# Seven sum levels instead of five and a single scale for the down weights in an attention + mixture-of-experts layer

## The reference, cut to what matters

```python
# B, T, C = 16, 512, 256; 16 heads of 16; 32 experts of width 128, top 8
x = layernorm(x + attention(x))        # q, k, v, rope, causal softmax, projection, biases
logits = x @ gate_w.T                  # x as (8192, 256)
top_w, top_idx = top_k(softmax(logits), 8)
top_w = top_w / top_w.sum(-1)
for e in range(32):                    # comb[t, e] = top_w where e is chosen, else 0
    g, u = split(x @ gate_up_w[e].T)
    acc += (u * silu(g)) @ down_w[e].T * comb[:, e]
out = layernorm(x + acc)               # layernorm without scale and bias
```

## Time and profile before

| | |
|---|---|
| runs | 2085.57, 2093.41, 2096.18 us; median 2093.41 |
| the profiled execution | 2096.7 us, of it 2094.9 from the first to the last instruction |
| mean granted TensorE clock | 0.950 of full speed |
| busy | PE 1763.9 us (84%), VectorE 1573.7 (75%), ScalarE 1288.3 (61%), GpSimd 1192.8 (57%) |
| DMA | 494.32 MB, 236 GB/s on the mean |

### The profile page before, as it was taken

The page is one execution under the profiler, slowest core; times in us unless marked ns, Lnnn a source line. Parts: engine busy times, 40 slices in busy tenths (PEclk is TensorE's granted clock), DMA queues, the critical chain, the costliest instruction groups (busy, mean ns, idle before and its releaser), DMA issues. The chain is left out here.

```text
span 2094.9 us, 54004 instructions
## 1 busy us (share of the span) xinstructions
PE 1763.9 (84%) x17245; PEld 1244.8 (59%) x17245; DVE 1573.7 (75%) x3519; ACT 1288.3 (61%) x2994; POOL 1192.8 (57%) x1158
## 2 busy tenths in 40 slices
PE   3899888988898889888987978988889889899960
PEld 2455544555455445454554868877767778788750
DVE  4788888887887888877875535745777679688887
ACT  1556665665565455554554857876767677787740
POOL 1002465446434654455444677777777777777770
PEclk8899999999999999999998989999999999999985
DMA  4455776677656665667754856778998899799966
GB/s 140 112 156 150 228 253 212 202 232 237 212 164 215 223 209 173 214 221 258 232 186 153 306 186 217 234 248 314 339 330 276 282 317 332 267 325 345 313 207 220
DMA packets 244743, 494.32 MB, mean 236 GB/s; under 512 B 46787, under 2 KB 150485, under 8 KB 235232
## 3 DMA queue, kind: packets, MB, share of 16 engines
q1 hardware_dynamic: 168256, 302.81, 46.3%
q0 software_dynamic: 54528, 159.49, 20.5%
q10 hardware_dynamic: 21696, 28.58, 4.0%
HBM read 279.66 MB, written 229.44 MB: 243 GB/s over the span
## 5 line engine op out<-in xcount | busy, mean ns | idle before, releaser
L1307 ACT ACTIVATE pT<-ps 128x512 f32<-128x512 f32 (+2 forms) x992 | 647.3, 694 | 331.0 <-PE ps L1090 253.7
L921 POOL DMA_INDIRECT x_sorted<-xhl,idx x512 | 520.2, 1016 | 469.4 <-DVE xhl L1745 229.2
L1659 DVE TENSOR_REDUCE mn<-ps 128x1 f32<-128x512 f32 (+3 forms) x704 | 412.2, 631 | 47.4 <-PE ps L1064 45.1
L1156 PE MATMUL ps<-pT,gu_hi 128*128 128x128 f16 (+1 forms) x1792 | 387.4, 238 | 60.7 <-ACT pT L1307 59.6
L1157 PE MATMUL ps<-pT,gu_hi 128*128 128x128 f16 (+1 forms) x1792 | 386.9, 237 | 0.0
L1158 PE MATMUL ps<-pT,gu_lo 128*128 128x128 f16 (+1 forms) x1792 | 379.6, 236 | 0.2 <-issue 0.2
L938 POOL DMA_INDIRECT y_tokens<-work,yidx x248 | 264.1, 1065 | 75.0 <-issue 55.3
L1062 PE MATMUL ps<-stacks 96*128 96x512 bf16 (+3 forms) x1024 | 271.9, 310 | 41.3 <-DMA stacks<-qk_parts 18.8
L1088 PE MATMUL ps<-stacks 99*128 99x512 bf16 (+3 forms) x1024 | 283.1, 306 | 24.8 <-ACT pT L1307 21.0
L1156 PEld LDWEIGHTS ps<-pT,gu_hi 128*128 x1792 | 176.5, 99 | 94.2 <-issue 73.1
L1090 PE MATMUL ps<-maskk,identb 128*128 128x128 bf16 x1024 | 221.6, 222 | 0.0
(11 more groups left out here) (235 smaller groups left out, 3610.8 us busy)
## 6 DMA issues: line engine op xcount, KB each, us to landing
stacks<-y_tokens SPq DMA_DIRECT2D x64, 1024.0 KB
stacks<-qk_parts SPq DMA_DIRECT2D x128, 192.0 KB
qk_parts<-pbuf SPq DMA_DIRECT2D x31, 768.0 KB, 4.5
stacks<-qk_parts SPq DMA_DIRECT2D x128, 128.0 KB
attention<-yev ACTq DMA_DIRECT2D x64, 256.0 KB
x_sorted<-pads_h SPq DMA_DIRECT2D x66, 160.0 KB
pT<-x_sorted SPq DMA_DIRECT2D x64, 160.0 KB
pbuf<-x_sorted SPq DMA_DIRECT2D x62, 160.0 KB
```

What stands on the lines that cost most here:

```text
L921: pool.indirect_dma_start(xsort[g][:, :], bass.IndirectOffsetOnAxis(ap=at, axis=0), xhl_rows[:, t, :], None).then_inc(s_scat, 16)
L1156: mmul(o, w_hi[k], x_hi[k], start=k == 0, stop=False)
L1307: return nc.scalar.activation(o, i, f, **k)
L1659: V.tensor_reduce(mn[:, tt, h0:h0 + nh], ps[:, odd_bank("max", at, m), 0:nh * n].rearrange("p (a n) -> p a n", a=nh), axis=AX.X, op=ALU.ma ...
```

## The change

- `LEVELS` has seven levels, of 4, 4, 2, 2 batches in group 0 and 2, 1, 1 in group 1. By `level_pairs` group 0 has 80 blocks of 256 rows instead of 112, group 1 16 as before; the 32 lie in the level of batches 8 to 11, whose blocks run in steps 72 to 104. The number of blocks and steps stays at 288 and 144. By `plan` the levels' first tiles come at steps 50, 82, 107, 120, 138, 148 and 153 instead of 50, 82, 114, 139 and 153, and the last tile at step 156 instead of 160.
- The down weights get one scale for all columns: VectorE takes the largest absolute value of each expert's rows (one more reduction in `measure`), multiplies the 32 by `mm` in iteration 8 and finds the largest of all with one transpose. ScalarE multiplies the rows by the scale (instead of VectorE). In the sums the two operations L1931 and L1934 become one.
- Batch 14's end, in iteration 15, has a table `LAST` of its own: numerators at place 3 (8 before), reciprocals out at 5 (6), division at 13 (12), inverse root at 13 (20), mean column 17 (20), normalisation 18 (22), x1's transposes 23 and 24 (24 and 25), the high and low copies of x1 both at 31 (26 and 29).
- The clears of group 0 go out in every other place of iterations 13 and 14.
- `first_row` of the table moves from x1T into `prep`, whose layout changes with it.

```diff
--- before.py
+++ after.py
@@ -88,11 +87,12 @@
...
 PREP_K = 2
+TOP = 16384.0
 
 
 BLK, UNIT = 256, 128
 GROUPS = ((0, 12), (12, 16))
-LEVELS = ((0, 4), (4, 8), (8, 12), (12, 14), (14, 16))
+LEVELS = ((0, 4), (4, 8), (8, 10), (10, 12), (12, 14), (14, 15), (15, 16))
 NG = len(GROUPS)
...
@@ -266,8 +266,11 @@
...
 
+LAST = dict(EACH, num=3, rec_out=5, divide=13, rsqrt=13, mean=17, norm=18, split=31, lower=31, x1=(23, 24), x1_out=(23, 24))
+
+
 def slots(i):
-    return LATE if i >= B else EACH
+    return LATE if i >= B else LAST if i == B - 1 else EACH
 
...
@@ -342,8 +345,8 @@
...
                         take(i, "gu", p + E * stage - 1)
-                    if stage == 1 and p in (2, 3):
-                        take(i, "fin", p - 2)
+                    if stage == 1 and p == 3:
+                        take(i, "fin", 0)
                 if place == 0 and (i, e) in TABLE_OUT:
...
@@ -470,7 +472,6 @@
...
         room, paired, sofar, twice, ended, ind, share = (eq[:, k * BINS[0]:(k + 1) * BINS[0]] for k in range(7))
-        first_row = eq[:, 7 * BINS[0]:8 * BINS[0] + 1]
         lane = sb("lane", [P, 5 * NLANE[0]])
...
@@ -486,12 +487,14 @@
...
 
-        prep = sb("prep", [P, 3 * C + 3 * E + 8])
-        mxd, rinvb, rwide = (prep[:, k * C:(k + 1) * C] for k in range(3))
-        mm = prep[:, 3 * C:3 * C + E]
-        mgu = prep[:, 3 * C + E:3 * C + 3 * E].rearrange("p (e m) -> p e m", e=E)
-        mx2 = prep[:, 3 * C + 3 * E:3 * C + 3 * E + 4].rearrange("p (r m) -> p r m", r=2)
-        rcp = prep[:, 3 * C + 3 * E + 4:3 * C + 3 * E + 8].rearrange("p (r m) -> p r m", r=2)
+        HEAD = 2 * C + 64 + BINS[0] + 8
+        prep = sb("prep", [P, HEAD + 3 * E + 8])
+        mxd, rwide = prep[:, 0:E], prep[:, C:C + P]
+        first_row = prep[:, 2 * C + 64:2 * C + 64 + BINS[0] + 1]
+        mm = prep[:, HEAD:HEAD + E]
+        mgu = prep[:, HEAD + E:HEAD + 3 * E].rearrange("p (e m) -> p e m", e=E)
+        mx2 = prep[:, HEAD + 3 * E:HEAD + 3 * E + 4].rearrange("p (r m) -> p r m", r=2)
+        rcp = prep[:, HEAD + 3 * E + 4:HEAD + 3 * E + 8].rearrange("p (r m) -> p r m", r=2)
         first_parts = pT[1][:, :, :].rearrange("p h t -> p (h t)").bitcast(BF16).rearrange("p (a r t) -> p a r t", r=2, a=3)
...
@@ -810,7 +810,7 @@
...
                         wait(sp, s_ys[k], stored(last_of(k, 2 * LEVEL_END[l])))
-                wait(sp, s_cmb, 7 * (q - NYG) + 3)
+                wait(sp, s_cmb, 6 * (q - NYG) + 3)
                 rows = ytok[q * P * TOPK:(q + 1) * P * TOPK, :].rearrange("(p k) c -> p k c", k=TOPK)
...
@@ -818,9 +818,9 @@
...
                     wait(sp, s_x1s, 16 * NB)
-                    wait(sp, s_rcb, 1)
+                    wait(sp, s_mid, 8)
                     wait(sp, s_dlo, E // 2)
-                wait(sp, s_cmb, 7 * (q - 2) + 5)
+                wait(sp, s_cmb, 6 * (q - 2) + 4)
                 sp.dma_start(x1r[:, q % 2, :], x1_dram[b, t * P:(t + 1) * P, :]).then_inc(s_x1r[q % 2], 16)
...
@@ -843,8 +843,9 @@
...
 
-                if i == GROUPS[0][1] + 1 and 0 <= e - SLOT_TAILS < E:
-                    clear_tail(0, e - SLOT_TAILS)
+                at = (i - NB + 3) * STEPS + e
+                if i < NB and 0 <= at < 2 * E and at % 2 == 0:
+                    clear_tail(0, at // 2)
                 if i >= NB and 0 <= (i - NB) * STEPS + e - LATE_TAILS < E:
...
@@ -1015,17 +1016,10 @@
...
                     xpose4(k, lambda j: rows_gu(n % 2)[:, j % 2, (j // 2) * P:(j // 2) * P + P]).then_inc(s_str, 1)
-                if stage == 1 and e in (2, 3):
-                    if e == 2:
-                        pe.wait_ge(s_dm, E)
-                        k = odd.take(s_mid, 1, "fin", 0)
-                    else:
-                        pe.wait_ge(s_mid, 4)
-                        k = odd.take(s_rb, 1, "fin", 1)
-                    src = (mxd, rwide)[e - 2]
-                    for j in range(2):
-                        last = nc.tensor.transpose(ps[:, k, j * P:(j + 1) * P], src[:, j * P:(j + 1) * P], ident[:, :])
-                    last.then_inc(s_fin, 1)
+                if stage == 1 and e == 3:
+                    pe.wait_ge(s_mid, 3)
+                    k = odd.take(s_mid, 5, "fin", 0)
+                    nc.tensor.transpose(ps[:, k, 0:P], rwide, ident[:, :]).then_inc(s_fin, 1)
 
...
@@ -1325,15 +1319,16 @@
...
                     actv(products(n, 1)[:, 0, :], rows_dn(n % 2), ACT.Copy, scale=mm[:, n:n + 1]).then_inc(s_dev, 1)
-                    if n >= 2:
-                        act.wait_ge(s_dm, n - 1)
-                    actv(sizes(n % 2), rows_dn(n % 2), ACT.Abs, scale=mm[:, n:n + 1]).then_inc(s_dev, 1)
                     if n + 2 < E:
-                        act.wait_ge(s_dev, 2 * n + 2)
+                        act.wait_ge(s_dev, n + 1)
+                        act.wait_ge(s_dm, n + 1)
                         load_rows(act, n + 2)
-                if stage == 1 and e == 3:
-                    act.wait_ge(s_fin, 2)
-                    actv(rinvb, ps[:, odd_bank("fin", 1), 0:C], ACT.Copy).then_inc(s_rb, 1)
+                n = e - 4
+                if stage == 1 and 0 <= n < E // 2:
+                    act.wait_ge(s_mid, 8)
+                    act.wait_ge(s_dev, E)
+                    wait(act, s_dlo, n - 1)
+                    actv(scaled(n % 2), products(2 * n, 2), ACT.Copy, scale=rinv[:, 1:2]).then_inc(s_dsc, 1)
                 n = e - 5
...
@@ -1572,6 +1567,9 @@
...
                     V.reciprocal(rcp[:, r, :], mgu[:, e, :]).then_inc(s_sv, 1)
+                    dve.wait_ge(s_drow[r], 16 * (e // 2 + 1))
+                    V.tensor_reduce(mxd[:, e:e + 1], rows_dn(r), axis=AX.X, op=ALU.max,
+                                    apply_absolute_value=True).then_inc(s_dm, 1)
                     V.scalar_tensor_tensor(out=mm[:, e:e + 1], in0=mgu[:, e, 0:1], scalar=4.0, in1=mgu[:, e, 1:2],
...
@@ -1585,31 +1583,24 @@
...
 
-                n = e + E * stage - 1
-                if 0 <= n < E:
-                    dve.wait_ge(s_dev, 2 * n + 2)
-                    if n > 0:
-                        dve.wait_ge(s_dm, n)
-                    V.tensor_tensor(mxd, sizes(n % 2), mxd if n else sizes(0), ALU.max).then_inc(s_dm, 1)
                 if stage == 1 and e == 2:
+                    dve.wait_ge(s_dm, E)
+                    dve.wait_ge(s_mm, E)
+                    V.tensor_tensor(mxd, mxd, mm, ALU.mult).then_inc(s_mid, 1)
+                    dve.wait_ge(s_mid, 1)
+                    V.tensor_reduce(rinv[:, 0:1], mxd, axis=AX.X, op=ALU.max).then_inc(s_mid, 1)
+                    dve.wait_ge(s_mid, 2)
+                    V.tensor_copy(rwide, rinv[:, 0:1].to_broadcast([P, P])).then_inc(s_mid, 1)
+                    V.tensor_scalar(mgh[:, :], mgu[:, :, 0], 0.5, None, ALU.mult).then_inc(s_mid, 1)
+                if stage == 1 and e == 3:
                     dve.wait_ge(s_fin, 1)
-                    V.tensor_reduce(rinv[:, :], ps[:, odd_bank("fin", 0), 0:C].rearrange("p (m f) -> p m f", m=NC), axis=AX.X,
-                                    op=ALU.max).then_inc(s_mid, 1)
-                    dve.wait_ge(s_mid, 1)
-                    V.tensor_scalar_max(rc[:, :], rinv[:, :], 1e-30).then_inc(s_mid, 1)
-                    dve.wait_ge(s_mid, 2)
-                    V.reciprocal(rinv[:, :], rc[:, :]).then_inc(s_mid, 1)
-                    dve.wait_ge(s_mid, 3)
-                    V.tensor_copy(rwide.rearrange("p (m f) -> p m f", m=NC), along(rinv[:, :], P)).then_inc(s_mid, 1)
-                    V.tensor_scalar(mgh[:, :], mgu[:, :, 0], 0.5, None, ALU.mult).then_inc(s_mid, 1)
-                n = e - 4
-                if stage == 1 and 0 <= n < E // 2:
-                    dve.wait_ge(s_rb, 1)
-                    if n == 0:
-                        V.reciprocal(rcb[:, :], rinvb).then_inc(s_rcb, 1)
-                    if n >= 2:
-                        dve.wait_ge(s_dlo, n - 1)
-                    V.tensor_tensor(scaled(n % 2), products(2 * n, 2), under(rinvb, 2), ALU.mult).then_inc(s_dsc, 1)
+                    V.tensor_reduce(rc[:, 0:1], ps[:, odd_bank("fin", 0), 0:P], axis=AX.X, op=ALU.max).then_inc(s_mid, 1)
+                    dve.wait_ge(s_mid, 5)
+                    V.tensor_scalar_max(rinv[:, 0:1], rc[:, 0:1], 1e-30).then_inc(s_mid, 1)
+                    dve.wait_ge(s_mid, 6)
+                    V.tensor_scalar(rc[:, 1:2], rinv[:, 0:1], 1.0 / TOP, None, ALU.mult).then_inc(s_mid, 1)
+                    dve.wait_ge(s_mid, 7)
+                    V.reciprocal(rinv[:, 1:2], rc[:, 1:2]).then_inc(s_mid, 1)
                 n = e - 5
...
@@ -1928,18 +1919,17 @@
...
                     wait(dve, s_cmb, at + 3)
-                    V.tensor_tensor(a, a, rcb[:, :], ALU.mult).then_inc(s_cmb, 1)
+                    wait(dve, s_x1r[r], 16 * (q // 2 + 1))
+                    V.scalar_tensor_tensor(out=a, in0=a, scalar=rc[:, 1:2], in1=x1r[:, r, :], op0=ALU.mult,
+                                           op1=ALU.add).then_inc(s_cmb, 1)
```

(15 more changed lines are left out.)

4 lines of the change are left out of this document (removed).

## The result

Twelve runs of the changed kernel have a median of 2082.95 us (2073.75 to 2098.53), twelve of the kernel before beside them 2094.53 (2085.57 to 2108.94). The ratio is 0.9924, 95% interval 0.9899 to 0.9949: 16 us faster, 11 to 21. The two medians alone lie 11.6 us apart, at the low end of that interval. Forecast were 26.

What follows compares the result with a forecast made beforehand. GpSimd's scatters were taken to bound the expert stretch, between attention and a tail of sums. Gains of 15.7 + 3 + 5.5 + 2 = 26.2 us from 2093.4 gave 2067 us, range 2048 to 2084.

Steps and rivals of the forecast that it cites:

- tail only: Rival, chance 0.24: attention savings come back as waits between PE, ScalarE and VectorE; only the tail's 15.7 us remain, 2078 us.
- line for faster: Whole kernel: a measurement tells about 0.5%, so faster means under 2083 us; chance 0.82.
- the signs: Trace marks: first gate about 1148 us, GpSimd gaps at most 0.3, last scatter 8 to 12 us earlier, no long tile waits.
- The tail: Token sums at the end: seven levels and one down scale gain 15.7 us, ends 11 and 19.
- Fewer 256-row blocks: Expert steps 72 to 104: 24 us more PE time, under GpSimd's 6.06 us a step; cost 0, at most 10.
- PE takes over: Rival, chance 0.08: PE sets the pace in steps 72 to 104, losing 11 or 24 us before cushion; 2090 us.
- Batch 14's places: Iteration 15: earlier numerators let the division start some 5 us earlier; gain 3 us, ends 0 and 7.
- Weight preparation: Attention iterations: less ScalarE and VectorE work gains 5.5 us in iterations 0 to 7, 2 in 9 to 12.
- GpSimd in the block stage: Expert blocks: GpSimd works without a pause, one scatter every 1.065 + 0.3 us, and hides time lost elsewhere.
- the slower rival: Rival, chance 0.06: scatters grow longer in steps 72 to 144; at +0.08 us each, 51 us lost, 2118 us.
- The clears: 32 issues on SP over two iterations instead of one: 0 us, ends -1.5 and 1.5.

Runs made afterwards that it cites:

- e2: Changed kernel with six levels, batches 8 to 11 as one level again; 2087.2 us, ratio to the kernel before 0.9928.
- e3: Changed kernel with batch 14's end at the places of all other batches; 2083.9 us, ratio to the kernel before 0.9924.
- e9: Kernel before with only the numerators of every batch read early, at place 5; 2064.9 us, ratio to the kernel before 0.985.
- e6: Changed kernel with every batch's numerators read at place 5 instead of 8, sine products in a free tile; 2040.3 us, ratio to the kernel before 0.9723.
- e5: Kernel before, unchanged, run and traced once more; 2102.3 us, ratio 1.0018.
- e4: Changed kernel with five old levels, batch 14's old places and old clears, so only the one down scale remains; 2098.8 us, ratio to the kernel before 0.9966.
- e10: e6 with six levels, batches 8 to 11 as one level; 2043.4 us, ratio to the kernel before 0.9737.
- e11: e6 with batch 14's end at the places of all batches; 2038.7 us, ratio to the kernel before 0.9729.
- e12: e6 with batch 14's numerators at place 3 instead of 5; 2039.6 us, ratio to the kernel before 0.972.

## Why the prediction was right, and where not

The measured 2083 us lie in the range (2048 to 2084), at its slow end, 16 us from the forecast's 2067; faster was right, since the interval of the ratio leaves 1 out. The range holds the result only because its slow end was taken from the rival "tail only"; and the forecast's own line for faster, under 2083, was met by 0.05 us. Of the signs, the first gate came at 1147.8 us as said, GpSimd had no longer gaps and no slower scatters, and VectorE no wait ahead of tiles 56 and 60; the last scatter came 7.1 us earlier, not 8 to 12.

**The tail (15.7 predicted): 15.3.** The sum was made from the start of tile 52 and put the end 37.4 us after the last scatter; it came 37.8 us after it. Sizes inside were off and cancelled: the fused operation takes 0.48 us, not 0.42, the pitch is 4.04, not 3.94, the wait for GpSimd's root was 3.42 and not 1.8 us; against that, tile 53 started 15.9 us before the last scatter and not 14.0. That the sum is right to 0.4 us is in part luck. What the prediction did not say is that two splits share the gain (e2).

**Fewer 256-row blocks (0): 0, but not for the reason given.** From ScalarE's copy for block 144 to that for block 208, steps 72 to 104, the kernels with 112 blocks of 256 rows took 190.8 to 196.5 us (eight traces, mean 194.2), those with 80 of them 198.6 to 202.6 (six, mean 200.2): 6.25 us a step. ScalarE's waits for PE's transposes there grew from 7.3 us (1584 to 1774 us in the kernel before) to 23.4 (1577 to 1767 in the changed one). So PE did not stay under GpSimd's 6.06; the measured 2.80 us a half step of thirteen other steps did not carry over. The Trainium skill ("TensorE: Matmul & The Clock Gate", section Back-to-back issue gap) gave the better estimate, 6.16. What made the 6 us cost nothing is the cushion: paired in order, copies and scatters of those steps came as close as 10.0 us before and 3.9 us after, and GpSimd ran dry in no trace. The rival "PE takes over" was right about which engine sets the pace there; it put the loss at 11 or 24 us ahead of the cushion, it was 6, and the cushion took all of it.

**Batch 14's places (3): some 1 to 3,** not resolved better than that (e3), with less at the division than thought (1.2 us earlier, not 5) since the issues put ahead of the row of maxima cost PE 2.8 us (0.5 before) and not 1.2.

**Weight preparation (5.5 and 2): 0. This is the step that failed.** The text counted what ScalarE and VectorE save, and asked what hides it among the engines of the same groups, but not which wait ends last in an iteration. That is the numerators' read. SP could issue it only when the rotation of the next q and k had left its buffer, behind the loads of stacks, and with DMA at 0.8 in the windows above. The savings are real (9 us in e9 against e6) and were given back in first groups: in iterations 9 to 12 by 0.2 us of idle time and 1.0 of lower clock each, against e5. That the lower clock follows from that wait is not shown; what is shown is that both went, and the 9 us came, when the read went out early. The rival "tail only", 2078 us, was right that the savings come back and that the tail and batch 14 alone remain: 15.3 and 1 to 3 us lie inside the measured interval of 11 to 21. The wait that it named, of PE, ScalarE and VectorE for each other in turn, was not the one: it is a read from DRAM.

**GpSimd in the block stage: right.** No gap over 0.35 us between first and last scatter in any of the fourteen traces, mean scatter 1.05 to 1.07 us, so the slower rival falls. The clears cost nothing that shows in B, which is 430.6 us in e3 and 430.9 in e4, the kernel with the old ones.

**Left open:** why the clock in iterations 1 to 7 falls in some first groups and not in others of the same trace, and why it falls further in iterations 9 to 12 with one scale. A first group at 0.83 to 0.85 is some 4 us longer than one at 1.00 (the figures are in the last section), so this may be much of the spread between runs of one kernel; no run shows how much.

## What to carry to other kernels

Before counting what an iteration saves, find the wait of that iteration that is set from outside, here a read that a shared buffer holds back; until that moves, time saved elsewhere can come back as idle time or a lower clock. One free tile that let the read go out 13 us earlier was worth more than twice the whole change. A stage behind a full queue hides lost time only as far as the queue is deep: measure the closest approach of producer and consumer, not their mean rates.

## What was not expected of the hardware

After a short idle time PE can run at the lower of its two clocks for a while, and that can cost more than the idle time. In iteration 5 of the changed kernel the first projections follow 1.71 us of idle time, and the same four matmuls take 1.91 us until the clock is back:

```profile
429.13 0.37 PE L1107 MATMUL ps<-spare,ones 65*128 65x256 bf16 x1 [1.71 <-DVE mn L1650]
429.30 1.91 PE L1109 MATMUL ps<-wpT,ynum 128*128 128x256 f32 x4
...
435.06 1.08 PE L1109 MATMUL ps<-wpT,ynum 128*128 128x256 f32 x4
```

In iteration 4, after 0.93 us, they take 1.03. Iteration 5's first group took 20.2 us at a granted clock of 0.83, iteration 4's 16.5 at 1.00: 3.7 us for 0.8 us of idle time. First groups of 1.00 granted clock (all matmuls at 2.4 GHz) took 16.5 to 17.7 us in the changed kernel and before, those of 0.83 to 0.85 (a part of them at 1.2 GHz) 20.2 to 22.4. It is no rule by length alone: a gap of 2.69 us in iteration 11 of the kernel before left the clock at 1.00, and after 0.80 us in both iterations 4 and 5 of e6 it was 1.00 in the one and 0.91 in the other. The Trainium skill (the same page, section HAM oscillation) tells of a kernel whose short bursts of matmuls each end in a wait for a DMA, so that each next burst starts at the low clock. The changed kernel agrees in part: in iterations 9 and 10 the first projection starts at the low clock after 2.98 and 3.67 us of waiting (0.37 us for a matmul that takes 0.27 at the full one), though only one such wait stands in each iteration, and groups two to four, 47 us of work, run at 1.00.

With the wait gone the kernel also became steadier: twelve runs of the changed kernel lie within 25 us, five of e6 within 5.4 and six each of e10, e11 and e12 within 8.7, 14.0 and 11.4.
